# Layer norm of the next 512-row window emitted before the RMS norm of the current one, with two buffers for the transposed window

## The reference, cut to what matters

```
x = x + attn(layernorm(x))
x = x + ffn(layernorm(x))          # silu(gate) * up, then down; quantized weights
def attn(x):
    q    = rmsnorm(x @ w_dq, g_q) @ w_uq         # 2048 -> 768 -> 16 heads * 192
    kv   = rmsnorm(x @ w_dkv, g_kv)              # 2048 -> 512
    k_nope, v = kv @ w_uk, kv @ w_uv
    k_pe = x @ w_kr                              # 2048 -> 64, then rope
    causal softmax over (q_nope k_nope + q_pe k_pe) / sqrt(192), times v, times w_o
```

## Time and profile before

| | us |
|---|---|
| time, median of 2 runs | 3762.94 (3675.6 and 3850.29) |
| the profiled execution's own time | 3687.11 |
| its span on the slowest core (core 5) | 3685.1 |
| spans of the other cores | 3639.3 to 3674.4 |
| TensorE busy with matmuls, share of the span | 57% |
| VectorE, ScalarE busy | 25%, 15% |
| the stage of the change on core 5, first x load to first matmul of the head groups | 79.6 to 758.3 |

### The profile page before, as it was taken

How to read it: one execution, slowest core, us unless ns; L and a number is a source line. 1 busy time by engine, 2 the same in 40 slices (tenths; PEclk the granted TensorE clock), 3 DMA queues, 4 the chain that set the end, 5 groups by cost and what they waited for, 6 DMA issues and landing times.

```text
span 3685.1 us, 26954 instructions; the slowest of 8 cores (3639.3 to 3685.1 us)
## 1 busy us (share of the span) xinstructions
PE 2113.3 (57%) x8330; PEld 795.5 (22%) x8330; DVE 911.1 (25%) x1224; ACT 559.0 (15%) x731; POOL 24.7 (1%) x36
## 2 busy tenths in 40 slices
PE   0311333255475557536753738678888888858645
PEld 0100111111121112202220213233333333323322
DVE  6122221144234333523451422200000010010011
ACT  1112112101240223023302322101000000000000
POOL 0000000000000000000000000000000000000000
PEclk9955666677697679757985878789999999979877
DMA  1322232300790098019603983333323323133333
GB/s 23 71 69 63 52 70 67 81 2 1 86 117 13 0 103 110 3 12 112 90 3 35 109 146 103 117 69 69 69 46 69 69 46 80 28 81 74 81 80 80
DMA packets 374105, 239.73 MB, mean 65 GB/s; under 512 B 344596, under 2 KB 355988, under 8 KB 366741
## 3 DMA queue, kind: packets, MB, share of 16 engines
q0 software_dynamic: 17936, 92.01, 20.3%
q1 hardware_dynamic: 356038, 146.00, 16.4%
HBM read 226.03 MB, written 85.98 MB: 85 GB/s over the span
## 4 chain that ended last, share of the span: by engine, by line
PE 50%; DVE 19%; DMA 11%; ACT 8%; issue 6%; another core or an unknown queue 2%; SPq 2%; DVEq 1%; ACTq 0%
PE ps_u__153 L991 4%; PE ps_u__152 L991 4%; PE ps_g__150 L991 4%; PE ps_g__151 L991 4%; DMA xst__34<-x_full 3%; DMA x1r__141<-x_scr 2%; ACT p_sb__73 L805 2%; SPq L75 2%; DVE act_sb__144 L1007 2%; DMA qpe_ext__66<-bnd_row__71 2%; DVE p_sb__73 L812 1%; DVE st__37 L335 1%; ACT hst__35 L352 1%; DVE rec_sb__74 L820 1%
## 5 line engine op out<-in xcount | busy, mean ns | idle before, releaser
L387 PE MATMUL ps_c__49<-hwin__38,wdkv_sb__45 128*128 128x512 bf16 x64 | 23.6, 551 | 358.9 <-DMA hwin__38<-hst__35 358.9
L812 DVE TENSOR_TENSOR p_sb__73<-p_sb__73,masks__17 128x512 bf16<-128x512 bf16 x256 | 108.8, 425 | 374.1 <-ACT p_sb__73 L805 371.4
L991 PE MATMUL ps_g__150<-h2T__129,slab__145 128*128 128x512 bf16 x704 | 163.8, 387 | 12.3 <-DMA slab__145<-g_scr 11.5
L991 PE MATMUL ps_u__152<-h2T__129,slab__146 128*128 128x512 bf16 x704 | 160.4, 381 | 3.2 <-issue 1.1
L991 PE MATMUL ps_g__151<-h2T__129,slab__145 128*128 128x512 bf16 x704 | 162.2, 384 | 0.0
L991 PE MATMUL ps_u__153<-h2T__129,slab__146 128*128 128x512 bf16 x704 | 159.8, 380 | 3.4 <-issue 0.2
L1007 DVE SCALAR_TENSOR_TENSOR act_sb__144<-ps_u__152,sup_c__8,gate_sb__147 128x512 bf16<-128x512 f32 x44 | 33.0, 751 | 519.8 <-PE ps_u__152 L991 519.8
L1051 PE MATMUL ps_d__156<-dslab__148,act_sb__144 128*128 128x512 bf16 x96 | 38.0, 396 | 140.3 <-DMA dslab__148<-d_scr 138.9
L1001 ACT ACTIVATE gate_sb__147<-ps_g__150,sgate_c__7 128x512 bf16<-128x512 f32 x44 | 30.2, 687 | 541.3 <-PE ps_g__150 L991 541.3
L335 DVE TENSOR_REDUCE st__37<-xst__34 128x1 f32<-128x2048 f32 x24 | 54.9, 2286 | 225.9 <-DMA xst__34<-x_full 160.8
L666 ACT ACTIVATE sqs__69<-kno__67 128x2048 bf16<-128x2048 bf16 x16 | 30.6, 1910 | 502.7 <-DVE vtok__68 L658 501.6
(11 more groups left out here) (474 smaller groups left out, 3596.9 us busy)
## 6 DMA issues: line engine op xcount, KB each, us to landing
g_scr<-wq_gate POOLq DMA_DIRECT2D x4, 5632.0 KB, 57.2
u_scr<-wq_up POOLq DMA_DIRECT2D x4, 5632.0 KB, 109.8
d_scr<-wq_down POOLq DMA_DIRECT2D x4, 5632.0 KB, 157.4
xst__34<-x_full SPq DMA_DIRECT2D x16, 1024.0 KB, 5.7
xst__34<-x_q SPq DMA_DIRECT2D x8, 1024.0 KB, 5.8
xqst__130<-x_q SPq DMA_DIRECT2D x8, 1024.0 KB, 5.5
wo_sb__128<-w_o POOLq DMA_DIRECT2D x2, 4096.0 KB, 40.4
x_scr<-x1st__131 SPq DMA_DIRECT2D x8, 1024.0 KB, 3.9
```

Of the source, the lines that this page charges most:

```text
L812: dep_v = QV.op(lambda v, pbuf=pbuf, midx=midx: v.tensor_mul(p_sb[:, pbuf:pbuf + 1, :], p_sb[:, pbuf:pbuf + 1, :], masks[:, midx:midx + 1, ...
L991: return t.matmul(pp[:, :], slab[sb_i][:, c:c + 1, hcl * 128:(hcl + 1) * 128], h2T[:, c:c + 1, nt * 512:(nt + 1) * 512], start=(c == 0), s ...
```

## The change

hwin grows from one window to two (32 blocks of 512 columns), and ln_tile gets the half to write to. The four ln_tile calls of a window become a helper, emit_ln4. The first window's layer norm is emitted ahead of the loop. Inside the loop the layer norm of the next window is emitted right behind the matmuls of the current one, that is ahead of its tail, on every queue. The last kv window emits the first q window's. The wait of SyncE is now for the matmuls that last read the same half.

```
-    hwin = al.sb("hwin", [128, 16, 512], BF16, side="right")
+    hwin = al.sb("hwin", [128, 32, 512], BF16, side="right")
...
-        d_tr = QS.dma(dT[buf], hwin[:, :, dst_col:dst_col + 128], ha, transpose=True)
+        d_tr = QS.dma(dT[buf], hwin[:, hb * 16:(hb + 1) * 16, dst_col:dst_col + 128],
+                      ha, transpose=True)
...
-    hwin_rd = 0
+    hwin_rd = {0: 0, 1: 0}
+
+    def emit_ln4(src, tile0, hb2):
+        QS.wait(tS, hwin_rd[hb2])
+        for j in range(4):
+            ln_tile(src[(tile0 + j) * 128:(tile0 + j + 1) * 128, :],
+                    j * 128, j % 2, hb2)
+
+    emit_ln4(x_full, 0, 0)
     for wdx in range(4):
         wc = wdx * 512
-        QS.wait(tS, hwin_rd)
-        for j in range(4):
-            d_hw = ln_tile(x_full[(4 * wdx + j) * 128:(4 * wdx + j + 1) * 128, :],
-                           j * 128, j % 2)
+        hb = wdx % 2
         QT.wait(dT[0], dT[0].n)
         QT.wait(dT[1], dT[1].n)
         QT.wait(dW, d_wkr)
         QT.wait(vS, vS.n)
...
-        hwin_rd = tS.n
-        QA.wait(tS, hwin_rd)
+        hwin_rd[hb] = tS.n
+        if wdx < 3:
+            emit_ln4(x_full, 4 * (wdx + 1), (wdx + 1) % 2)
+        else:
+            emit_ln4(x_q, 0, 0)
+        QA.wait(tS, hwin_rd[hb])
...
     for wdx in range(2):
         wc = wdx * 512
-        QS.wait(tS, hwin_rd)
-        for j in range(4):
-            d_hw = ln_tile(x_q[(4 * wdx + j) * 128:(4 * wdx + j + 1) * 128, :],
-                           j * 128, j % 2)
+        hb = wdx % 2
...
-        hwin_rd = tS.n
-        QA.wait(tS, hwin_rd)
+        hwin_rd[hb] = tS.n
+        if wdx == 0:
+            emit_ln4(x_q, 4, 1)
+        QA.wait(tS, hwin_rd[hb])
```

More of the change, by code:

```diff
@@ L326, in build_nc, with ln_tile @@
     h_last_rd = [0, 0]
-    def ln_tile(src_rows, dst_col, buf):
+    def ln_tile(src_rows, dst_col, buf, hb):
         xa = xst[:, buf:buf + 1, :]
@@ L385, in build_nc, with mm @@
             for c in range(16):
-                def mm(t, m=m, c=c):
+                def mm(t, m=m, c=c, hb=hb):
                     return t.matmul(ps_c[m][:, :],
                                     wdkv_sb[:, c:c + 1, m * 128:(m + 1) * 128],
-                                    hwin[:, c:c + 1, :],
+                                    hwin[:, hb * 16 + c:hb * 16 + c + 1, :],
                                     start=(c == 0), stop=(c == 15))
@@ L392, in build_nc, with mm1, mm2 @@
         for c in range(16):
-            def mm1(t, c=c):
+            def mm1(t, c=c, hb=hb):
                 return t.matmul(ps_kp1[:, :], wkr_sb[:, c:c + 1, 0:32],
-                                hwin[:, c:c + 1, :],
+                                hwin[:, hb * 16 + c:hb * 16 + c + 1, :],
                                 start=(c == 0), stop=(c == 15))
-            def mm2(t, c=c):
+            def mm2(t, c=c, hb=hb):
                 return t.matmul(ps_kp2[:, :], wkr_sb[:, c:c + 1, 32:64],
-                                hwin[:, c:c + 1, :],
+                                hwin[:, hb * 16 + c:hb * 16 + c + 1, :],
                                 start=(c == 0), stop=(c == 15))
```

## The result

The changed kernel takes 3564.64 us in the median (11 runs, 3551.46 to 3768.85); the kernel before, on the same chip, 3690.95 us (10 runs, 3675.36 to 3899.92). The ratio is 0.967, with a 95% interval of 0.9643 to 0.9697: 3.3% faster. The forecast was 3561.5. (Some executions of every kernel are disturbed on one die; the ratios leave these out, the medians over all runs do not.)

What follows compares the result with a forecast made beforehand. In the stage before the first projections, TensorE's wait for the layer norm was taken as the bound. The terms summed to -125.6 us, so 3687.1 became 3561.5 us, 3.4% less, with a range of 3530 to 3620.

Steps and rivals of the forecast that it cites:

- Terms 1 and 2: Matmuls hidden in five windows, -117.3 us; landing of the last transposes hidden behind the tail, -35.1 us.
- Term 3: Between the first window's last transpose issue and the next load there is now that issue, +2.0 us.
- Terms 4 and 5: The q windows' layer norms take 119.1, not 114.9, +4.2 us; matmuls wait some 7 us for w_dq, cost 0.
- Term 6: Kv and first q tails: 22 squaring steps at TensorE's slow clock after idling, 0.8 us each, +17.6 us.
- Term 7: Second window's loads follow the first's at once and may collide: one slow tile, +3 us, at most 11.9.
- Term 8: Layer norm beside dense matmuls costs nothing, 0 us; from above 6 us a window, 30 in all.
- A: Rival: layer norms run at the first window's pace, 68.4 us each; time 3612 us, chance 0.06.
- B: Rival: layer norm transfers beside busy TensorE become as slow as beside a weight load; time 3732 us, chance 0.04.
- C: Rival: the tail too is hidden under the next layer norm, 24.2 us in five windows; time 3441 us, chance 0.02.
- D: Rival: a later stage, candidate feed-forward, waits for something that doesn't move; time up to 3687 us, chance 0.04.

Runs made afterwards that it cites:

- e2: Changed kernel's queue order with a single hwin buffer in place of two; 3686.53 us, ratio 0.9975 to the kernel before.
- e3: The change in the first three kv windows only, q windows keeping the layer norm in front of their matmuls; 3612.2 us, ratio 0.9775.
- e7: Changed kernel plus 164 unneeded matmuls behind each kv window's own and 124 behind the first q window's; 3549.55 us, ratio 0.9639.
- e4: Changed kernel with each tile's x load issued one tile earlier in SyncE's queue; 3469.35 us, median of four runs, no ratio drawn.
- e8: Changed kernel with x loads issued one tile ahead, run again with more runs; 3409.91 us, ratio 0.9245 to the kernel before.
- e1: Changed kernel plus 150 unneeded matmuls behind each kv window's own and 140 behind the first q window's; 3708.73 us, six runs, no ratio.

## Why the prediction was right

By its own steps, on core 5 unless said otherwise:

- **The order of the work.** The walk through the queues gave layer norm 56.5 + tail 24.2 + 0.7, with 3.2 more for the clock: 84.6. It is 84.9, and the parts stand where they were put: TensorE released by VectorE, the layer norm 0.7 us behind the matmuls' start, the tail begun 0.02 us after the last transpose's issue. e2 shows that the second buffer is the condition, e3 that the windows add up.
- **Terms 1 and 2**, -152.4: hidden. The head groups' mean start moved by 124.5 for a sum of 125.6.
- **Term 3**, +2.0: the first window's last issue took 1.93 us, with the next load 0.08 us behind it.
- **Terms 4 and 5.** The layer norm beside the w_dq load took 489.50 to 552.11, 62.6 us, as forecast. The matmuls started at 505.41, 26.5 us after the load's issue, and the layer norm beside them ran for 24 us after they ended; 22.7 was the cover forecast. Cost 0. But the wait itself was misread: the sign was matmuls some 7 us behind the end of the tail, and they came 16.6 us behind it (488.82 to 505.41). The rows of before already say so: the tail ended near 532 and not near 542, as the next load at 532.98 shows, and the weights landed at 549.3. The cost stayed 0 because the end of the matmuls hangs on the landing of the weights, not on the end of the tail.
- **Term 6**, the clock: forecast +17.6 by steps of 2.7 to 2.8, measured 0.85 x 22 = 18.7. All 22 pairs of the five tails took 1.87 us in place of 1.02, on each of the eight cores. On core 5 two slow pairs of before, in its third tail, had already cost 1.6 of this (1.78 and 1.87 in place of 1.02), so the change added 17.1. The Trainium skill, "TensorE: Matmul & The Clock Gate", Part 1, lets activity release the clock, and by that rule half the steps might have been fast again. They were not, in any of 176 steps, with TensorE busy for 7.46 of 11.60 us in a tail. Where the extra matmuls kept it busy up to the tail, the later steps were 1.91 (e7).
- **Term 7** was sized too high: the layer norm right behind the first one took 57.5 us (58.1 on core 4), so +1.0 to 1.6 and not +3. This and the first window itself, 2.1 us shorter in this execution, are why core 5 reached the head groups at 628.10 and not at 632.7.
- **Term 8**, 0: layer norms beside matmuls took 56.2 to 57.8 us, and 57.4 beside a TensorE that never paused (e7).
- **The rivals.** A (68.4 us a layer norm) and B (slow transfers, 82 us and more) fall with 56.2 to 57.8. C (the tail hidden too) falls with squares that never start ahead of the last transpose's issue. D falls with an end that came over 120 us earlier and a wait for slabs of 13.7 us, against 12.3 of before.

What follows the stage is not equally long on all cores and in all executions: from the head groups to the end core 5 took 2926.9 us before and 2916.8 after, core 4 took 2909.7 and 2932.0. That is why the slowest core changed. In the mean of the eight cores it was 2906.2 us before and 2915.9 after, so in these two executions about 10 of the 124.5 us did not reach the end. The causes of these 10 to 20 us were not looked into. That the forecast lies within 4 us of the median is closer than this scatter allows for, and in so far luck; the steps of the stage are not.

## What to carry to other kernels

A wait in an in-order queue holds everything behind it: walk each engine's queue in the new order, and the length of the cycle is the sum of what can't be passed. A second buffer does nothing while the wait for the first stands ahead of the next load (xst here, until e4), and a new order does nothing without the second buffer (hwin, e2). When one wait is removed, price the next cycle with the lengths of the old rows, and then ask the wait table which part of it is again only a wait: here SyncE's 293.0 us pointed to e8, the version that is 7.6% faster than before and beats both kernels.

## What was not expected of the hardware

- The clock did not come back in any tail that began with it at 0.50, though pairs of matmuls kept TensorE busy for two thirds of the time. Before, such a step was seen in one tail; now it is all five that follow a layer norm.
- How the clock falls is not told by the gap alone. In e1 a tail on core 5 that began 1.12 us after the last extra matmul had one pair of 1.02 us, one of 1.67 and two of 1.86; in e7 on core 2 one that began after 1.18 us had only pairs of 1.02, and one after 2.02 us a pair of 1.02 and three of 1.86. In the third tail of before, on core 5, the clock fell after only 0.89 us of idle time ahead of the tail, with pairs of 1.02, 1.02, 1.78 and 1.87. No bound for the gap is drawn from that.
- Transfers of a layer norm at twice the density cost next to nothing here: in e8 the DMA engines moved 205 GB/s from 186 to 214 us, in after 102 GB/s from 233 to 290 us, and the transposes were issued in 1.6 to 2.2 us in both. A load of x_full landed 6.2 us after its issue in e8 and 5.9 in after (core 5, medians, 80 to 600 us).
